# First self-attention's staging: the projection of a batch set ahead of the next batch's normalisation, and the first unit's maxima behind the last projection

## The reference, cut to what matters

```python
q = rope(proj(wq, bq))
k = rope(proj(wk, bk))
v = proj(wv, bv)
score = jnp.einsum('bhqd,bhkd->bhqk', q, k) / math.sqrt(HEAD_DIM)
...
x = x + _L0_attn_ref(_layernorm(x, axis=-1), L0_attn_wq, ...)
```

## Time and profile before

| | us |
|---|---|
| median of 3 runs | 853.66 |
| lowest and highest of them | 847.53, 855.85 |
| the profiled execution | 858.58 |
| span of the profiled execution, first to last instruction | 856.4 |
| PE busy, share of the span | 82% |
| DVE busy, share of the span | 69% |

### The profile page before, as it was taken

The page is one execution under the profiler, slowest core; times in us unless marked ns, Lnnn a source line. Parts: engine busy times, 40 slices in busy tenths (PEclk is TensorE's granted clock), DMA queues, the critical chain, the costliest instruction groups (busy, mean ns, idle before and its releaser), DMA issues.

```text
span 856.4 us, 14952 instructions
## 1 busy us (share of the span) xinstructions
PE 699.2 (82%) x4698; PEld 336.8 (39%) x4698; DVE 591.0 (69%) x1606; ACT 415.0 (48%) x708; POOL 283.8 (33%) x504
## 2 busy tenths in 40 slices
PE   2479999989889998309999992459799998999787
PEld 1244454444434444205666561213233232324443
DVE  3767677786645664637788872688889898962664
ACT  1313565655664534102333330318688877886454
POOL 4633454553531323731323221122433034230220
PEclk9867999998976756658999996759999999999999
DMA  7542654383231312411111113520212210000000
GB/s 215 171 150 89 204 163 154 118 256 101 82 88 52 96 37 79 124 53 35 39 45 40 42 36 105 171 74 26 87 64 87 87 52 26 26 2 1 0 26 25
DMA packets 74780, 71.27 MB, mean 83 GB/s; under 512 B 14560, under 2 KB 67168, under 8 KB 74704
## 3 DMA queue, kind: packets, MB, share of 16 engines
q1 hardware_dynamic: 72000, 64.84, 24.4%
q0 software_dynamic: 2272, 4.69, 1.7%
q10 hardware_dynamic: 432, 0.79, 0.3%
HBM read 41.90 MB, written 28.00 MB: 82 GB/s over the span
## 4 chain that ended last, share of the span: by engine, by line
PE 62%; DVE 17%; issue 10%; ACT 4%; DMA 3%; POOL 2%; SPq 2%; DVEq 0%; POOLq 0%; ACTq 0%
PE bank_pv L732 11%; DVE mx L590 9%; PE bank_turn L574 8%; PE bank_scores L2023 5%; PE bank_scores L684 4%; PE bank_scores L1773 4%; PE bank_turn L1758 4%; PE bank_scores L1758 4%; PE bank_turn L751 3%; PE bank_scores L1766 2%; PE bank_turn L528 2%; PE bank_turn L793 2%; DVE xn L471 2%; PE bank_turn L578 1%; PE bank_turn L835 1%
## 5 line engine op out<-in xcount | busy, mean ns | idle before, releaser
L590 DVE TENSOR_REDUCE mx<-bank_turn 128x1 f32<-128x512 f32 (+3 forms) x452 | 260.7, 616 | 68.5 <-PE bank_turn L579 35.1
L574 PE MATMUL bank_turn<-stk 64*128 64x77 bf16 (+4 forms) x708 | 163.4, 313 | 30.0 <-DVE mx L590 21.1
L684 PE MATMUL bank_scores<-stk 64*128 64x512 bf16 (+4 forms) x576 | 177.6, 374 | 4.8 <-ACT probs L705 3.6
L709 ACT ACTIVATE probs<-bank_scores 128x1024 f32<-128x1024 f32 (+4 forms) x160 | 117.4, 768 | 104.2 <-PE bank_scores L684 102.5
L705 ACT ACTIVATE probs<-bank_scores 128x512 f32<-128x512 f32 x256 | 138.6, 605 | 35.1 <-PE bank_scores L684 34.2
L732 PE MATMUL bank_pv<-probs,vsl 128*32 128x512 f32 (+4 forms) x1152 | 146.8, 584 | 2.8 <-POOL probs L717 1.8
L574 PEld LDWEIGHTS bank_turn<-stk 64*128 64x128 bf16 x708 | 54.5, 102 | 135.4 <-DVE mx L590 65.7
L717 POOL TENSOR_SCALAR_AFFINE_SELECT probs<-probs 128x256 f32<-128x256 f32 x128 | 51.9, 409 | 80.3 <-ACT probs L709 78.9
L1741 POOL DMA_INDIRECT expert_outputs<-probs,y_at x39 | 37.3, 957 | 106.2 <-DVE probs L1660 103.3
L528 PE MATMUL bank_turn<-ident,xn 128*128 128x128 f32 x60 | 14.7, 391 | 62.8 <-DVE xn L471 62.7
L477 POOL TENSOR_TENSOR rstd<-var,mhalf 128x4 f32<-128x4 f32 x24 | 25.4, 1057 | 117.5 <-DVE var L456 117.2
(11 more groups left out here) (299 smaller groups left out, 1189.2 us busy)
## 6 DMA issues: line engine op xcount, KB each, us to landing
stk<-stack_A SPq DMA_DIRECT2D x64, 256.0 KB, 3.3
w<-in_M_w SPq DMA_DIRECT2D x12, 512.0 KB, 5.0
stack_A<-parts SPq DMA_DIRECT2D x15, 384.0 KB, 2.8
stack_A<-fill SPq DMA_DIRECT2D x8, 512.0 KB, 5.6
stk<-stack_X SPq DMA_DIRECT2D x16, 256.0 KB, 2.7
stack_A<-parts SPq DMA_DIRECT2D x15, 256.0 KB, 3.2
probs<-routed_tokens SPq DMA_DIRECT2D x39, 65.0 KB, 1.8
b_gated<-in_M_b SPq DMA_DIRECT2D x1, 2048.0 KB, 10.8
```

The lines of the kernel that those rows point to most:

```text
L574: mm = e.matmul(o, stk[r, slot, 0, pp, qt * P:(qt + 1) * P], stk[r, slot, 1, pp, 0:keys], start=True, stop=not a.causal)
L590: e.tensor_reduce(o.rearrange("p h q -> p q h"), bank_of((g, m))[:, 0:k * keys].rearrange("p (q h k) -> p q h k", q=len(tiles), h=len(hs)) ...
L684: mm = e.matmul(score_bank(g, kt, i)[0:a.kp, 0:S - q0], stk[r, slot, 1, pp, kt * P:kt * P + a.kp], stk[r, slot, 0, pp, q0:S], start=True, ...
L709: e.activation(probs[0:a.kp, probs_of(g, kt), j:HG:2, 0:n], bank_scores[0:a.kp, 2 * j:2 * j + 2, 0:n], ACT.Exp, scale=1 / math.sqrt(HD)).t ...
```

## The change

On PE, batch b+1 is projected before batch b+2 is turned, and the maxima of unit 0 come after all four projections. DVE, ACT and POOL follow: DVE projects batch b+1 before it normalises b+2, ACT's copy of xnT(b+2) moves from ahead of batch b+1's copies to the place between its first casts and its second ones, and neg_of for unit 0 leaves POOL's loop over the batches. The diff, whole but for context:

```diff
@@ stage0_act (ACT), between the first casts and the second
+            if b in (1, 2):
+                norm_act(e, 0, b + 1)
             for z in range(2):
                 e.wait_ge(s["rest"], 2 * b + z + 1)
@@ first_stream_pe
             stage0_pe(e, 0)
+            stage0_pe(e, 1)
             norm_pe(e, 0, 2)
-            stage0_pe(e, 1)
+            stage0_pe(e, 2)
             norm_pe(e, 0, 3)
-            stage0_pe(e, 2)
+            stage0_pe(e, 3)
             all_maxima_pe(e, 0)
-            stage0_pe(e, 3)
             turn_pe(e, 0)
@@ first_stream_dve
             rest0_dve(e, 0)
+            stage0_dve(e, 1)
             normalise(e, 0, 2)
-            stage0_dve(e, 1)
             moments_dve(e, 0, 3)
             rest0_dve(e, 1)
+            stage0_dve(e, 2)
             normalise(e, 0, 3)
-            stage0_dve(e, 2)
             rest0_dve(e, 2)
-            all_maxima_dve(e, 0)
             stage0_dve(e, 3)
+            for k in range(len(A0.items)):
+                max_dve(e, 0, k)
+                if k == 3:
+                    rest0_dve(e, 3)
             turn_dve(e, 0)
-            rest0_dve(e, 3)
             all_maxima_dve(e, 1)
@@ first_stream_act
             stage0_act(e, 0)
-            norm_act(e, 0, 2)
             stage0_act(e, 1)
-            norm_act(e, 0, 3)
@@ first_stream_pool
                 bias_pool(e, A0, b)
                 if b == 0:
                     values_pool(e, 0)
-                if b == 2:
-                    neg_of(e, 0)
+            neg_of(e, 0)
             neg_of(e, 1)
```

## The result

| | before | after |
|---|---|---|
| median, 20 runs each | 854.02 us | 849.36 us |
| lowest to highest | 846.88 to 860.11 | 841.08 to 857.09 |
| profiled execution, its span | 856.4 | 844.2 |

The ratio after to before is 0.9947, with a 95% interval of 0.9921 to 0.9972: 2 to 7 us faster, 0.5%, within the 1% that I counted as no change. The forecast was 847.6, 6.1 us faster than the median of the first three runs before; the medians of 20 runs lie 4.7 us apart.

The account below looks back on a forecast made before the run. It took the staging to be bound by a ring: project, split, normalise the next, turn, project. Unit 1's maxima starting at 65.3 instead of 71.43 save 6.1 us: 853.66 - 6.1 gives 847.6, range 840.5 to 855.

Parts of the forecast that it names:

- Bound and direction: Staging: PE idles 6.64 us before each turn of xn(2) and xn(3); removing this makes the kernel 6.1 us faster.
- xnT(3) waits for a DMA: ACT's copy of xnT(3) stands behind batch 2's cast of k, which now waits for k of stack(1) to land.
- the first rival: The DMA doesn't hold xnT(3): landing at most 44.6, 8.5 to 9.2 us saved, time 844.8; chance 0.10.
- The landing: k of stack(1) lands at 47.0, between 44.6 (beside the loads) and 47.9 (behind them).
- PE's row starts 0.24 ahead of the copy: PE's first projection row starts 0.24 us before ACT's xnT copy; used to place stage0(2) and stage0(3), the latter at 47.45.
- The clock over stage0(3): stage0(3) on PE takes the same 6.1 us as stage0(2) before, at low clock, since PE again comes out of idleness.
- the rival of a high clock: The clock stays up over stage0(3): up to 2.2 us more, 8.3 saved, time 845.4; chance 0.13.
- stage0(3) and the maxima, the wait for neg: Unit 0's maxima take 8.3 us, batch 3's remainder adds 1.4, the new wait for POOL's neg 1.45 before unit 1's maxima.
- From there to PE's first score both versions have the same instructions, paced by DVE: From unit 1's first maximum to the first score 5.3 us either way, with 13 maxima in 6.54 us without a gap.
- The sum: Unit 1's maxima start at stage0(3)'s row plus 17.9, 65.3 against 71.43: 6.1 us saved through to the end.
- given back on the spot: Rival: stack(1) lands later still, at 49.8; 3.2 us saved, or about 2, time 851; chance 0.17.
- Slower by the clock: Rival: PE enters unit 0 at low clock and stays so longer; 4 us slower, 857.6; chance 0.08.

Follow-up runs that it names:

- e1: Changed kernel, but ACT copies xnT(3) ahead of batch 2's first casts instead of behind them; ratio 0.9910 to the kernel before.
- e2: Changed kernel with a second buffer for the split parts of batches 1 and 3; ratio 0.9894 to the kernel before.
- e8: Changed kernel, but SP loads only units 0 and 1 ahead of stack(1), units 2 and 3 behind it; ratio 0.9893 to the kernel before.
- e5: Changed kernel with two parts buffers, batch 3's remainder behind unit 0's maxima and neg ahead of batch 3's third parts; ratio 0.9874 to the kernel before.
- e10: Changed kernel with units 2 and 3 loaded behind stack(1) and batch 3's remainder behind unit 0's maxima; ratio 0.9906 to the kernel before.
- e6: Changed kernel with two parts buffers and unit 0's maxima put back between stage0(2) and stage0(3); ratio 0.9839 to the kernel before, median 840.63 us.
- e7: Changed kernel with batch 3's remainder behind unit 0's maxima and neg ahead of batch 3's third parts; ratio 0.9973 to the kernel before, median 852.14 us.

## Why the prediction was right, and where its terms were off

- *Bound and direction*: right. PE's wait for xn fell from 6.64 us to 4.75 and 1.93, and the gain at the first score passed on to the end, within what 20 runs can tell: 3.5 us of 854 is a ratio of 0.9959, inside both intervals of the changed kernel. The size was not right: 6.1 us forecast, 3.5 measured at the first score. That the median came within 1.8 us of the forecast (849.36 against 847.6) shows little, since single runs vary by 10 and more.
- *xnT(3) waits for a DMA*: right, and it decided the case. Without this step the forecast would have been 8.5 us or more, the first rival, at the edge of "faster". e1 took the copy out from behind the wait, e2 removed the wait, e8 shortened it, and each moved the copy.
- *The landing* ("I take 47.0"): 1.1 us too early. The cast of k came at +22.3, where I had +21.2. I expected the 3.8 us earlier issue to remove a pause of 1 us between the loads and the stack; k of stack(1) landed at +22.3 all the same, 0.2 us ahead of before. The late end of my bounds (47.9, or +22.0) was the better one. The Trainium skill (DMA: Bandwidth & Descriptors, "Queues, rings and completion order") states that each DMA engine takes the descriptors of a ring in order. The trace agrees: no DMA of stack(1) landed before the last load, and from issue to landing they took 5.8 to 6.3 us in the median of each size, where they took 2.9 to 3.0 before.
- *"PE's row starts 0.24 ahead of the copy"*: this step failed. I read stage0(2) at 46.00 against the copy of xnT(3) at 46.24. But stage0(2) reads xnT(2), which was copied 14 us earlier; the two rows only stand beside one another. A real successor, after, starts 0.63 behind the copy's start (49.58 to 50.21). From the copy to unit 0's first maximum it is 7.5 us and not 6.5; 0.9 of the difference is this step.
- *The clock over stage0(3)*: right, the low clock: granted 0.58 from 50.21 to 54.7, and DVE's first three cosine instructions of batch 3 come 1.71 and 0.91 apart, as in batch 2 before (1.66 and 0.86, from 47.95). So the rival of a high clock falls for the changed kernel, in both its profiles. But with the pause gone the clock can stay up: in e1 and e5, where PE stood idle for 0.7 us instead of 4.60, it was 1.00 over stage0(3), and in e5 the first maximum came 5.7 us behind the copy instead of 7.5. In e2, e8 and e10, with a pause of 0.7 to 0.9, the low clock came back (7.4 us). What decides between the two is not shown.
- *stage0(3) and the maxima, the wait for neg*: 11.15 forecast from unit 0's first maximum to unit 1's, 10.7 measured. The gap ahead of the third maximum was shorter (0.60, not 0.91), with PE's rows at 0.22 us a matmul and not 0.31, and the remainders covered another of 0.20. The wait for neg was longer than forecast: 1.78 us from the last maximum's end (66.02) to unit 1's first, not 1.45.
- *"From there to PE's first score both versions have the same instructions, paced by DVE"*: true of the instructions, not of the pace. Before, PE filled three banks while DVE did batch 3's remainder, and 13 maxima ran without a gap. Now PE starts unit 1 with DVE waiting, and behind unit 1's first maximum DVE has gaps of 0.43 and 0.29. Those 13 maxima take 7.55 us instead of 6.54, and the first score comes 6.35 us behind the first of them instead of 5.33. This step had the overlap wrong.
- *The sum*: 6.1 less 1.0 for the copy's later start (+22.9, where I had +21.8), less 1.1 for copy to maximum, plus 0.5 between the first maxima, less 1.0 for the lead, is 3.5, as measured. In size this is the rival "given back on the spot" (3.2), but only the first 1.0 is of its kind, a later landing; it had the landing at 49.8, which is +23.9, and it came at +22.3.
- *Slower by the clock*: did not happen. In the 50 us behind the first score the granted clock is 0.90 before and 0.89 after. The clock's variation of about 10 us lies 150 us and more behind the first score, and it is there before the change too.

## What to carry to other kernels

When a step is brought forward, check each wait on its new path that cost nothing so far, above all waits for a buffer whose last reader is a DMA, and ask what stands ahead of that DMA in its queue. Read a producer's row against its true consumer by the buffer's name; two rows 0.2 us apart may have nothing to do with one another. Measure a change of a few us at instants counted from a common event: where a landing sets them they repeated within 0.5 us here, and within 1.7 where the clock of a projection does, while the whole time varies by 10. When work is moved into a wait, look at what runs beside it there: it may lengthen the wait that it fills. The version to keep is one of those without the wait: e6 has the lowest ratio (0.9839, of 6 runs), e5 the earliest first score, e8 needs no buffer; their intervals overlap, so which is best stays open.

## What the runs showed of the hardware that I had not expected

- The stack of batch 1, issued 3.8 us earlier but directly behind 2 MB of loads, landed at about the same instant (k at +22.3 against +22.4). With half of the loads ahead of it the cast that waits for it came 3.7 us earlier.
- Two short POOL instructions (neg, 128x16) took 0.49 and 0.54 us beside DVE's remainders in e7, 0.20 and 0.22 alone in the changed kernel.
- The granted clock between about 235 and 405 us differs between executions of kernels with the same program there, and with it the time from the first score to the end: 770 to 780 us. What sets it was not tried.
